# Layer norm of the evacuated images in pairs on ScalarE, the convolution in two slots, attention loads first in their slot, third parts later

## What is computed

```python
x = x + 0.5 * ffn(layernorm(x), w12, w3, router_w, expert_bias, sw1, sw2, sw3)
x = x + attention(layernorm(x), qkv_w, conv_w0, conv_b0, conv_w1, conv_b1, proj_w, proj_b, ln_w, ln_b)
x = x + 0.5 * ffn(layernorm(x), w12, w3, router_w, expert_bias, sw1, sw2, sw3)

# ffn: a shared gated expert for every row, and 2 of 8 routed experts chosen by a sigmoid score
shared_out = silu(x @ sw1.T) * (x @ sw2.T) @ sw3.T
# attention: windows of 8 tokens, heads of 8 channels, in two branches (rows and columns)
lepe = conv_general_dilated(vimg, cw, ...)             # a 3-tap convolution of v, per channel
attn = softmax(part(q) * scale @ swapaxes(part(k), -1, -2))
out = attn @ vw + lepe                                 # then proj, its own norm, and the residual
```

## Time and profile before

| | |
|---|---|
| median of 3 runs | 1499.05 us (1496.1 to 1500.58) |
| the profiled execution, its own time | 1487.33 us |
| its span, first to last instruction | 1485.6 us |
| mean granted clock of TensorE | 0.997 of full speed |
| PE busy | 1410.1 us, 95% |
| DVE, ACT, POOL busy | 959.1, 545.5, 506.1 us |

### The profile page before, as it was taken

The page is one execution under the profiler, slowest core; times in us unless marked ns, Lnnn a source line. Parts: engine busy times, 40 slices in busy tenths (PEclk is TensorE's granted clock), DMA queues, the critical chain, the costliest instruction groups (busy, mean ns, idle before and its releaser), DMA issues.

```text
span 1485.6 us, 21823 instructions
## 1 busy us (share of the span) xinstructions
PE 1410.1 (95%) x7494; PEld 678.8 (46%) x7642; DVE 959.1 (65%) x1295; ACT 545.5 (37%) x1141; POOL 506.1 (34%) x424
## 2 busy tenths in 40 slices
PE   4999989999999899899998999999999999999998
PEld 2444444444444444445544444444444444444443
DVE  5777853333448989988889899978925732333333
ACT  4666323333233333345534454345233213333211
POOL 2221122221245574442625443444412122221353
PEclk9999999999999999999999999999999999999999
DMA  9999658887583665075525462355338158888595
GB/s 308 306 352 312 256 157 193 196 190 180 200 264 105 218 196 152 30 239 128 157 71 177 137 181 74 111 167 138 110 110 238 64 163 220 192 194 183 184 298 190
DMA packets 233724, 272.63 MB, mean 184 GB/s; under 512 B 132242, under 2 KB 156818, under 8 KB 230162
## 3 DMA queue, kind: packets, MB, share of 16 engines
q1 hardware_dynamic: 198594, 166.34, 39.0%
q10 hardware_dynamic: 23664, 67.66, 14.2%
q0 software_dynamic: 11360, 37.23, 9.3%
HBM read 168.39 MB, written 72.88 MB: 162 GB/s over the span
## 4 chain that ended last, share of the span: by engine, by line
PE 67%; DVE 9%; issue 5%; DMA 3%; POOL 3%; ACT 1%; SPq 0%; POOLq 0%; ACTq 0%; DVEq 0%
PE bank L1451 28%; PE bank L1465 14%; PE bank L1570 13%; PE bank L1595 7%; DMA rows<-sorted_y,slots 2%; PE side L1108 2%; DVE rows L575 1%; PE side L1583 1%; DVE region L1135 1%; DVE region L1141 1%; POOL hs L1776 1%; DVE sgh L1817 1%; POOL conv_tmp L1207 1%; POOL region L1209 1%; PE side L1238 1%
## 5 line engine op out<-in xcount | busy, mean ns | idle before, releaser
L1451 PE MATMUL bank<-xT,wb 128*128 128x512 bf16 x2607 | 605.9, 381 | 34.5 <-DMA xT<-region 17.6
L1451 PEld LDWEIGHTS bank<-xT,wb 128*128 128x128 bf16 x2688 | 256.3, 98 | 326.4 <-issue 30.6
L1776 POOL TENSOR_TENSOR hs<-sgh,hs 128x512 bf16<-128x512 f32 x126 | 162.4, 1289 | 631.5 <-ACT hs L1670 631.4
L1465 PE MATMUL bank<-wb,hs 128*128 128x512 bf16 x1510 | 353.3, 380 | 4.5 <-POOL hs L1776 2.9
L1465 PEld LDWEIGHTS bank<-wb,hs 128*128 128x128 bf16 x1536 | 148.6, 98 | 180.7 <-POOL hs L1776 6.5
L1570 PE MATMUL bank<-wr,region 128*128 x913 | 222.0, 379 | 5.3 <-issue 4.1
L1670 ACT ACTIVATE hs<-sgh 128x512 bf16<-128x512 f32 x128 | 80.9, 632 | 358.8 <-DVE sgh L1817 352.9
L1817 DVE TENSOR_TENSOR sgh<-bank,sgh 128x512 f32<-128x512 f32 x128 | 87.9, 687 | 150.0 <-PE bank L1451 149.7
L1135 DVE TENSOR_TENSOR region<-region 128x1024 f32<-128x1024 f32 x128 | 182.1, 1445 | 1.0
L1765 POOL DMA_INDIRECT region<-xnd,idxs x78 | 74.2, 951 | 225.0 <-DMA region<-region 220.4
L1141 DVE TENSOR_REDUCE region<-region 128x256 f32<-128x2048 f32 x64 | 146.3, 2286 | 2.2
(11 more groups left out here) (178 smaller groups left out, 1353.3 us busy)
## 6 DMA issues: line engine op xcount, KB each, us to landing
wb<-wsplit ACTq DMA_DIRECT2D x42, 1024.0 KB, 6.0
wb<-wsplit ACTq DMA_DIRECT2D x42, 512.0 KB, 4.2
sorted_y<-region SPq DMA_DIRECT2D x78, 256.0 KB
wsplit<-wb SPq DMA_DIRECT2D x8, 1536.0 KB, 7.5
wr<-wall SPq DMA_DIRECT2D x6, 1536.0 KB, 9.7
rows<-x SPq DMA_DIRECT2D x32, 256.0 KB, 4.8
region<-xln SPq DMA_DIRECT2D x128, 64.0 KB, 3.3
xnd<-rows SPq DMA_DIRECT2D x30, 256.0 KB, 4.3
```

The costliest lines, as they stand in the source:

```text
L1451: m = e.matmul(ps[:], wb[:, w % 2, wp, at:at + P], xt[:, xp, c, :], start=(i == 0), stop=(i == 3 * NDC - 1))
L1465: m = e.matmul(psD[tt][:], hs[:, s % 2, hp, tt * P:(tt + 1) * P], wb[:, w % 2, wp, at:at + D], start=(first and i == 0), stop=(last and i ...
L1776: e.tensor_tensor(hs[:, s % 2, 1, :], sgh[:, s % 2, :], hs[:, s % 2, 0, :], ALU.subtract).then_inc(S("h_lo").sem, 1)
```

## The change

1. The layer norm of an evacuated image is spread over slots `at` to `at + 3`, in two pairs of tiles: statistics of pair k in slot `at + 1 + k`, and in slot `at + 2 + k` a small shift on DVE (-mean times rstd, 128x1), the normalisation on ACT (Identity with scale and bias) and the store. The normalisation of 128x512 on DVE is gone. The combines of tiles 8 to 15 and one load (`EV_LOAD[3]`) stand two slots later. `spare` counts the new work, and the planner moves a few scores and values.
2. `pool_conv` is cut after its third instruction; the last two run in the next slot.
3. `Half(h).sp_load` for h of 1 and more stands first in its slot on SP's queue: ahead of the slot's stores and loads of rows, of which a store waits for DVE's result.
4. For the 12 tiles of images 0 to 2, `third` moves from place 2 to place 4 of its slot and the logits from place 5 to place 1 of the next slot.

```diff
@@ Evac
-                if self.ln:
-                    for tt in range(TI):
-                        e.wait_ge(S("ev").sem, 4 * v + tt + 1)
-                        row_stats(e, o, T(tt), 4 + tt, "ev_var")
-
-            def pool_rstd(self, e):
-                for tt in range(TI):
+
+            def vec_stats(self, e, o, k):
+                for tt in (2 * k, 2 * k + 1):
+                    e.wait_ge(S("ev").sem, 4 * self.v + tt + 1)
+                    row_stats(e, o, T(tt), 4 + tt, "ev_var")
+
+            def pool_rstd(self, e, k):
+                for tt in (2 * k, 2 * k + 1):
                     pool_root(e, 4 + tt, "ev_var", "ev_rstd", 4 * self.k + tt)
 
-            def vec_norm(self, e):
-                for tt in range(TI):
+            def vec_shift(self, e, k):
+                for tt in (2 * k, 2 * k + 1):
                     e.wait_ge(S("ev_rstd").sem, 4 * self.k + tt + 1)
+                    shift(e, 4 + tt).then_inc(S("ev_shift").sem, 1)
+
+            def act_norm(self, e, k):
+                for tt in (2 * k, 2 * k + 1):
+                    e.wait_ge(S("ev_shift").sem, 4 * self.k + tt + 1)
                     e.wait_ge(S(f"ev_stored{tt}").sem, EV_STORED[self.v] - 16)
-                    e.tensor_scalar(T(tt), T(tt), mv[:, 4 + tt, 0:1], rstd[:, 4 + tt, :], ALU.subtract,
-                                    ALU.mult).then_inc(S("ev_ln").sem, 1)
+                    e.activation(T(tt), T(tt), ACT.Identity, bias=mv[:, 4 + tt, 0:1], scale=rstd[:, 4 + tt, :]).then_inc(
+                        S("ev_ln").sem, 1)
...
@@ tables
-                    TILE.append((at - 1, at, at + 1, at + 2, at + 3, (at + 4, 2), (at + 4, 5)))
+                    TILE.append((at - 1, at, at + 1, at + 2, at + 3, (at + 4, 4), (at + 5, 1)))
...
+            left -= sum(2.1 * (0 <= s - at - 1 < 2) + 0.3 * (0 <= s - at - 2 < 2) for at, ev in zip(EV_AT, EVACS) if ev[4])
...
-        COMBINE_SLOT += [2 * UNIT + 3 + m for m in range(8)]
+        COMBINE_SLOT += [2 * UNIT + 5 + m for m in range(8)]
...
@@ pool_conv
-                for tap, a, b in ((0, slice(1, WL), slice(0, n)), (2, slice(0, n), slice(1, WL))):
+                if half == 0:
+                    o.do(e.tensor_tensor(to, v, weight(1, WL), ALU.mult))
+                    o.sync()
+                for tap, a, b in ((0, slice(1, WL), slice(0, n)), (2, slice(0, n), slice(1, WL)))[half:half + 1]:
...
@@ SP, slot(s), at its front
+                    for h in range(1, HALVES):
+                        if s == LOAD_SLOT[h]:
+                            Half(h).sp_load(e)
...
@@ ACT, slot(s), behind the rounding to hs
+                    for ev, k in evac_ln_at(s - 2):
+                        ev.act_norm(e, k)
...
@@ DVE, slot(s), behind vec_sum
-                    for ev in evac_ln_at(s):
-                        ev.vec_norm(e)
+                    for ev, k in evac_ln_at(s - 2):
+                        ev.vec_shift(e, k)
+                    for ev, k in evac_ln_at(s - 1):
+                        ev.vec_stats(e, o, k)
```

38 lines of the change are left out of this document (20 added, 18 removed).

## The result

| | before | after |
|---|---|---|
| median, 18 runs each | 1496.95 us (1488.13 to 1503.52) | 1489.86 us (1484.2 to 1497.63) |
| ratio to before | | 0.9958, 95% interval 0.9943 to 0.9972 |
| profiled execution, span | 1487.33, 1485.6 us | 1486.62, 1484.9 us |
| DVE, ACT, POOL busy | 959.1, 545.5, 506.1 us | 945.5, 553.7, 499.0 us |

The account below looks back on a forecast made before the run. PE bounds the kernel, busy 95% of the span, with DVE the second load; 3.2 + 1.4 + 1.3 + 1.8 - 1.5 + 5.6 + 4.2 + 1.0 = 17.0 us takes 1499.05 to 1482, range 1474 to 1494.

Parts of the forecast that it names:

- DVE becomes the bound sooner: Rival: where PE's wait goes, DVE's next product is due earlier; gain 5 to 12 us, about 1490; chance 0.26.
- Slower: Rival: third parts at place 4 put ACT's copy behind hs, delaying PE's logits; at 2.0 us a tile, 1506; chance 0.07.
- Slots 33 to 35, 41 to 44, 48 to 50: PE's waits for DVE's product, POOL's hs, a half's load and the silu shrink: gains 3.2, 1.3 plus 1.8, 5.6.
- Slot 37: DVE ends the merge about as much earlier as PE arrives: gain 1.4 us, bounds 0 and 1.4.
- Slots 45 and 46: New wait: the merge of half 1 comes late for the earlier PE; loss 1.5 us, bounds 0 and 4.
- Slots 65 to 68: Waits for DVE's product and the silu go, with 0.3 of POOL's hs: gain 4.2 us, bounds 1.5 and 4.2.
- Slots 91 to 95, +1.0: Third-part wait of 1.28 goes, about 1.1 given back; 0.7 for hs goes: gain 1.0 us, bounds 0 and 4.
- The load, +1.8: Slot 44: the half's load, issued ahead of slot 42's combine store, comes earlier; gain 1.8 us, bounds 0.5 and 2.2.
- The convolution, 1.3 and 1.0: Split lets POOL's hs start earlier: 1.3 us at slot 41; 0.7 at slot 95 within slots 91 to 95's 1.0.

Follow-up runs that it names:

- late sums: Kernel after with third parts back, DVE's two sums of each combine in slots 37 to 44 behind the slot's first attention work: 1482.9 us, 0.9923.
- the stores first: Kernel after, third parts back, all eight combine sums behind attention work, SP's eight attention-output stores ahead of the combine's store: 1478.59 us, 0.9885.

## Why the forecast was wrong

The direction was right and the gain more than twice too large. The time missed by 8 us only, since the three runs that 1482 was counted from lay 2 us above the median of 18. The rival "DVE becomes the bound sooner" (5 to 12 us, about 1490) has the number, and it named the merge of half 1, with the clock behind it, and slots 66 to 68. But 6.3 of the 11 us that are missing stand at slots 71 to 80 and 92 to 99, which it didn't name; the third parts were the rival "Slower". That its number fits is in part luck. By the steps of the sum:

- *Slots 33 to 35, 41 to 44, 48 to 50* held: 3.4, 3.2 and 5.5 us against 3.2, 3.1 and 5.6. Reading who waits at the end of a queue and shifting it by the work removed was enough there. Slot 37 gave 1.4, but PE now waits 0.76 us for the silu of slot 40.
- *Slots 45 and 46*: the step that failed was the overlap: "DVE's work has shrunk by 3.3", with all of it counted as time won. Its busy time up to the end of that merge fell even more, by 5.9 us (122.19 and 116.33 below, before and after, with columns as in the earlier trace rows):

```profile
460.68:592.24 131.56, 122.47 (x622) 58.51 (x634) 122.19 (x113) 46.89 (x128) 75.36 (x54) 1.00 0.57 183
466.65:596.22 129.57, 125.14 (x635) 59.91 (x646) 116.33 (x114) 49.81 (x132) 73.76 (x54) 1.00 0.61 187
```

  But DVE's waits in the same time add up to 12.5 us, against 8.6 before: it idles 3.23 us in slot 35, whence the combine had moved, and waits for gathers. From silu 32 to its end the merge took 596.21 - 466.65 = 129.6 us against 592.23 - 460.68 = 131.6: 2.0 us less, not 3.3. So PE waited 2.42 us and the lower clock took 1.7 more. The prediction had named gathers, with a loss of 4, as its bound. The kernels with earlier combines and with late sums show it: in both the wait is under 0.5 us.
- *Slots 65 to 68*: 2.85 of 4.2, and 0.5 given back in slot 70. DVE waited for PE 1.66 us in slot 65 (none there before), which I had not counted, and then worked to slot 69 with one pause of 0.32 us; so 0.86 us of the waits for the silu are left.
- *Slots 91 to 95, +1.0*: the largest error, with slots 71 to 80, where I had put 0. The move of the third parts costs instead of gaining: 2.5 us at slots 71 to 80 by the planner's move and logits behind ACT's copy, and in all 5.8 us by the ratios with and without it (4.8 on the kernel before), 3.9 and 2.6 by the slots where the edit moves something. I had read the planner's moves in the order of instructions and given them no price. Slot 98 has another cause: DVE has no pause from slot 92 on, so what PE wins there is waited for at the merge. That wait is 2.26 us with the third parts back too, and none with the norms alone or with norms and loads, where the convolution is whole and PE lost 0.78 us to POOL's hs just ahead; with a whole convolution and the later third parts it is 1.12. So the split has a share in it, the whole of it once the third parts are back, and the prediction had the gain of the split there (0.7) without that price.
- *The load, +1.8*: right for its place, and mis-sized as a part. I asked what the loads move past, not what the change puts ahead of them: without the move the norms' stores hold up half 3's loads (3.69 us of wait, 6.6 in slots 51 to 56), and in slot 44 PE, now early, waits 5.33 us. With the norms in the kernel the move is worth 8.4 us by the stretches.
- *The convolution, 1.3 and 1.0*: the waits for hs went as forecast and came back as waits for merges.

Not settled: what share of slot 98's wait is POOL's contention, and why the ratios give the third parts more than the slots do.

## What to carry over

Work taken from a busy engine is won only up to its next wait: sum its idle time over the stretch before and after, beside its work, and see whether a moved item leaves a hole behind. A planner's move is an edit like any other and has a price in the slot it leaves. When a queue gets new entries that wait, ask what stands behind them; test the parts of a change one by one, since here one part hid a loss of 8 us in another, and one cost 3 to 6.

## What the runs showed of the hardware

**DVE and POOL keep each other waiting.** Timelines of slot 24, where the change has moved nothing, same instructions: before,

```profile
397.72 0.75 DVE L680 SCALAR_TENSOR_TENSOR rows<-rows,coef 128x512 f32<-128x512 f32 x1
398.53 1.17 POOL L1776 TENSOR_TENSOR hs<-sgh,hs 128x512 bf16<-128x512 f32 x1
```

and with the third parts back,

```profile
397.75 1.91 DVE L689 SCALAR_TENSOR_TENSOR rows<-rows,coef 128x512 f32<-128x512 f32 x1
...
397.92 1.17 POOL L1795 TENSOR_TENSOR hs<-sgh,hs 128x512 bf16<-128x512 f32 x1
```

The same sum takes 0.75 us before POOL's hs starts and 1.91 beside it, 1.16 more, as long as hs itself (1.17). Reductions with one operand show nothing of the kind (L1141 before: mean 2286 ns in every run). It goes the other way too, and which of the two waits can change from one execution to another. DVE's attention product and the convolution's first instruction start within 0.01 us of each other in slot 66; before,

```profile
789.09 2.59 POOL L1204 TENSOR_TENSOR region<-region,cw 128x512 f32<-128x512 f32 x1
...
789.10 1.21 DVE L1135 TENSOR_TENSOR region<-region 128x1024 f32<-128x1024 f32 x1
```

and with the third parts alone on the kernel before, where nothing in slots 65 and 66 has moved:

```profile
793.27 1.49 POOL L1204 TENSOR_TENSOR region<-region,cw 128x512 f32<-128x512 f32 x1
...
793.28 2.57 DVE L1135 TENSOR_TENSOR region<-region 128x1024 f32<-128x1024 f32 x1
```

Once POOL's takes 1.10 us more, once DVE's 1.36; a second product behind it takes 0.8 more, and PE's wait in slot 68 is 2.2 us longer. The Trainium skill ("SBUF — State Buffer", SBUF: two separate sides) says that GpSimd and VectorE share a pair of ports under an exclusive lock, held for a whole instruction, which a VectorE operation with two SBUF inputs needs; whichever starts first has it, and the other waits. The traces agree in this, that one of the two waits for about the whole of the other. That the first to start wins can't be read from them: POOL's record starts 0.01 us ahead in both of slot 66, and DVE's 0.17 us ahead where it waited in slot 24.

**The same wait, with and without the lower clock.** PE waited 2.42 us in slot 79 in after and in the run with earlier combines. Busy time by stretch from there, after,

```profile
897.40:901.80 4.40, 4.14 (x23) 2.21 (x25) 3.52 (x6) 2.01 (x11) 2.03 (x3) 1.00 0.02 4
```

and with earlier combines:

```profile
894.60:899.00 4.40, 4.00 (x16) 1.98 (x18) 1.90 (x4) 1.34 (x10) 1.63 (x2) 0.61 0.00 0
```

1.00 (the higher level, 2.4 GHz) and 0.61 (between it and the lower, 1.2 GHz), with the same instructions ahead on PE: 4.4 x 0.39 = 1.7 us, and slots 75 to 80 take 44.4 and 46.1 us. At the merge of slot 98, 2.26 us went with 0.65 in after and with 1.00 with the stores first. So a wait of 2.3 us may cost 1.7 more or nothing, and a forecast should carry both.
